# First attention of a two-layer kernel: the next batch's key pieces placed in odd steps only, two or three in a row

## The reference, cut to what matters

```
def _L0_xattn_ref(x, y, ...):                       # y = ctx, x = layernorm(x)
    y_dca, y_main = y[:, -16:, :], y[:, :-16, :]
    k_dca = _ln(...); v_dca = ...                   # from y_dca @ Wkv_dca
    q = _ln((x @ Wq + bq).reshape(b, s1, 16, 16), qn_w, qn_b)
    k = _ln(y_main @ Wk + bk per head, kn_w, kn_b); v = y_main @ Wv + bv
    ctx     = softmax(q k^T * 0.25) v               # 16 heads of 16
    ctx_dca = softmax(q k_dca^T * 0.25) v_dca
    return (ctx + ctx_dca) @ Wo + bo
```

## Time and profile before

| what | value |
|---|---|
| median of three runs | 1445.93 us |
| profiled execution, its own time | 1445.58 us |
| its span, first to last instruction | 1444.2 us |
| mean granted TensorE clock | 0.956 |
| PE busy | 1328.7 us (92%) |
| DVE busy | 1083.1 us (75%) |
| ACT busy | 894.2 us (62%) |
| POOL busy | 700.1 us (48%) |

### The profile page before, as it was taken

One profiled execution on the slowest core, in us unless ns is written; L12 is line 12 of the kernel. 1 busy time (PEld: TensorE's weight loads), 2 busy tenths in 40 slices (PEclk: granted clock), 3 DMA queues, 4 the chain that ended last, 5 costly groups with the idle time before them and its releaser, 6 DMA issues.

```text
span 1444.2 us, 25271 instructions
## 1 busy us (share of the span) xinstructions
PE 1328.7 (92%) x8652; PEld 646.2 (45%) x8652; DVE 1083.1 (75%) x2323; ACT 894.2 (62%) x1575; POOL 700.1 (48%) x785
## 2 busy tenths in 40 slices
PE   5798998889889899789999999999999999999999
PEld 4343444344333344335454544445454545454445
DVE  6767788688797357767877776967778888888766
ACT  4746756657765756466666666656665556656554
POOL 4036243334140046157655557665577565556643
PEclk9788998999989999899999999999999999999999
DMA  4000400301250100001000000000010000000000
GB/s 179 1 1 5 84 8 14 57 2 20 52 206 1 60 1 7 23 24 30 1 1 1 23 2 24 6 1 24 1 30 30 1 30 1 30 1 1 1 2 30
DMA packets 20486, 36.68 MB, mean 25 GB/s; under 512 B 4898, under 2 KB 15238, under 8 KB 19334
## 3 DMA queue, kind: packets, MB, share of 16 engines
q1 hardware_dynamic: 20358, 35.07, 8.3%
HBM read 26.53 MB, written 1.15 MB: 19 GB/s over the span
## 4 chain that ended last, share of the span: by engine, by line
PE 48%; DVE 4%; issue 3%; ACT 2%; POOL 2%; DVEq 0%; POOLq 0%; ACTq 0%
PE BK L740 47%; DVE arena L1715 2%; POOL arena L2178 1%; ACT arena L2014 1%; PE BK L1391 1%; DVE arena L2367 0%; DVE arena L2373 0%; DVE BK L1740 0%; ACT arena L2026 0%; ACT L1034 0%; POOL arena L1117 0%; POOL arena L2169 0%; PE BK L1064 0%; ACT arena L2399 0%; POOL arena L1115 0%
## 5 line engine op out<-in xcount | busy, mean ns | idle before, releaser
L740 PE MATMUL BK<-arena 128*128 128x512 bf16 (+11 forms) x8322 | 1286.2, 359 | 72.4 <-DVE arena L1553 21.1
L740 PEld LDWEIGHTS BK<-arena 128*128 128x128 bf16 (+7 forms) x8322 | 612.1, 104 | 709.4 <-issue 206.8
L2178 POOL TENSOR_TENSOR arena<-arena 128x512 bf16<-128x512 f32 (+1 forms) x416 | 441.9, 1067 | 226.9 <-ACT arena L2014 175.3
L2014 ACT ACTIVATE arena<-BK,arena 128x512 f32<-128x512 f32 (+1 forms) x416 | 285.7, 687 | 186.8 <-PE BK L740 183.0
L1910 ACT ACTIVATE arena<-BK 128x512 f32<-128x512 f32 (+1 forms) x416 | 222.8, 601 | 108.4 <-PE BK L740 106.0
L1553 DVE TENSOR_REDUCE arena<-BK 128x1 f32<-128x512 f32 x384 | 240.7, 681 | 51.2 <-PE BK L740 50.6
L1740 DVE TENSOR_TENSOR BK<-BK,arena 128x512 f32<-128x512 f32 (+1 forms) x352 | 243.7, 692 | 16.1 <-ACT arena L2014 10.4
L1715 DVE CUSTOM_DVE_ANT_0 arena<-BK,arena 128x512 bf16<-128x512 f32 (+1 forms) x256 | 147.0, 574 | 102.4 <-PE BK L740 99.2
L2026 ACT ACTIVATE arena<-BK 128x512 bf16<-128x512 f32 (+1 forms) x256 | 129.5, 508 | 90.0 <-PE BK L740 88.8
L1766 DVE SCALAR_TENSOR_TENSOR arena<-BK,arena 128x256 f32<-128x256 f32 x128 | 55.8, 476 | 15.0 <-PE BK L740 15.0
L2077 POOL TENSOR_TENSOR arena<-arena 128x1024 f32<-128x1024 f32 (+2 forms) x15 | 23.3, 1551 | 89.1 <-DVE arena L1495 89.1
(11 more groups left out here) (188 smaller groups left out, 888.0 us busy)
## 6 DMA issues: line engine op xcount, KB each, us to landing
arena<-arena SPq DMA_DIRECT2D x144, 50.0 KB, 2.2
arena<-in_ctxT SPq DMA_DIRECT2D x8, 800.5 KB, 4.6
arena<-in_ctxk SPq DMA_DIRECT2D x4, 768.0 KB
arena<-in_wo SPq DMA_DIRECT2D x1, 2048.0 KB, 7.5
arena<-in_wqT SPq DMA_DIRECT2D x1, 2048.0 KB, 8.7
arena<-in_x SPq DMA_DIRECT2D x4, 256.0 KB, 9.9
arena<-in_rsel SPq DMA_DIRECT2D x1, 1024.0 KB, 9.6
arena<-in_rw1T SPq DMA_DIRECT2D x1, 1024.0 KB, 5.2
```

The lines of the kernel that those rows point to most:

```text
L740: return T.matmul(out_, lhsT, rhs, start=start, stop=stop, skip_group_check=True)
L2014: A.activation(P1[k][0:m, :], BK[i][0:m, :], ACT.Exp, scale=SCALE1, bias=mcb[0:m, b, kt:kt + 1]).then_inc(free[i], 1)
L2178: G.tensor_tensor(Pl[k][0:m, :], P1[k][0:m, :], Ph[k][0:m, :], ALU.subtract).then_inc(p_low, 1)
```

## The change

The pieces of `keyed` are given in odd steps only. A quota grows by 1.5 per step up to step 29 and by 1 afterwards; odd steps spend all of it. Steps 1 to 29 so take three pieces each instead of two, and the even ones none instead of one; from step 30, two and none instead of one and one. The number of pieces given by the end of each odd step is what it was.

```
+        quota = 0
         for s in range(-LEAD0, 16 * NKT + LAG0):
...
                 b = s // 52
-                for _ in range(1 + s % 2 if s < 30 else 1):
+                quota += 1.5 if s < 30 else 1
+                while quota >= 1 and s % 2 == 1:
+                    quota -= 1
                     next(keyed, None)
                 if b + 1 < B and s % 6 == 3:
                     next(valued[b + 1], None)
```

## The result

The changed kernel takes 1452.26 us (median of 20 runs, 1446.73 to 1454.68), the kernel before in the same session 1441.43 us (20 runs, 1436.9 to 1449.38). The ratio, which is taken from the means, is 1.0065, 95% interval 1.0053 to 1.0078: some 9.4 us slower, between 7.6 and 11.2 (the medians lie 10.8 us apart). The prediction was +0.7 us, no change. Executions of one and the same kernel lie several us apart, so a single profile shows where time goes, and only many runs show how much.

What follows compares the result with a forecast made beforehand. PE was taken as the bound (busy 92% of the span), with DVE full in some windows. -5.3 + 2.5 + 1.5 + 1.5 + 0.5 = +0.7 us gave 1446.6 us; range 1440.6 to 1452.8, the forecast's own 1443.5 to 1449.

Steps and rivals of the forecast that it cites:

- Rival (c): Slower: PE reaches group 7 no earlier, something else replacing the wait for rows; +6.0 us, 1451.9 us; chance 0.05.
- (b): Faster: seven banks let PE run over late ACT or DVE, losses cost 1 instead of 6.0 us; 1441.6 us; chance 0.26.
- credit for the clock behind it: Behind group 7's removed stall, 4.32 us at clock 0.50 would run at 1.00, saving 2.2 us.
- part 2: Batch 1, three key tiles in a row: PE's stalls at steps 24 and 30 grow, +2.5 us.
- part 4: Root steps behind `oD` delay the row maxima PE waits for: +1.5 us in batch 3, +0.5 in batch 2.
- part 3: Paired key tiles: step 80's slip counted at group 7; batch 3's SP chain shifts, group 11's wait grows, +1.5 us.
- part 1: Batch 2: six key DMAs go behind group 7's bounce, so PE's wait and half clock there vanish, -5.3 us.
- nothing else: Instructions unchanged in number and size; `kk`, `q`, `qr` move where PE is full; bank shifts cost nothing, +-1 us.
- Rival (a): Slower: longer stalls at steps 24, 30 and 109 bring half clock, 5 to 7 us, near 1452 us; chance 0.27.
- its own mark: Two of steps 24, 30 and 109 show clock 0.50 over some 4 us that were at 1.00 before.

Runs made afterwards that it cites:

- `nw 3 2` alone: Kernel before with only one root step, three DVE instructions, moved from ahead of `oD` to behind it (steps 108 and 109): 1444.36 us, ratio 1.002.
- kernels without SP's backlogs: Second-half key DMAs of batches 2 and 3 held behind group 7's and 11's bounces: on the kernel before 1431.51 us (0.9929), on the changed kernel 1445.6 us (1.0028).

## Why the prediction was right or wrong

**The number.** The measured 1452.26 us lies within the stated range, 1440.6 to 1452.8, and outside the forecast's own, 1443.5 to 1449. That the wide range holds it is luck: the range was built on 1445.93 us, and counted from the 1441.43 us of the 20 runs it would end near 1448. The forecast, no change, did not come true: the kernel is 9.4 us slower.

**What held.** Which stalls the change touches, and their lengths, came out point by point: SP's order with its 42 DMAs, the end of group 7's wait, and 2.71, 3.16, 2.48 and 3.86 us for the stalls that it said would grow. The 4.60 us for group 11's rows is the number that it gave, but kernels with the old order there have it too. Rival (c), a wait that stays at group 7, fell, and so did (b): no bank hid any of it.

**The step that failed: pricing a longer stall by its own length.** The sum gave the removed stall a credit for the clock behind it, 2.2 us, and gave the added ones no such charge. The kernels with one part each show the size of that:

| term | predicted | stall grew by | measured |
|---|---|---|---|
| part 2, batch 1's key tiles | +2.5 | 2.4 | 5.8 us (3.0 to 8.5) |
| part 4, batch 3's root steps (104 to 115) | +1.5 | 1.8 | 4.9 us (2.7 to 7.1) |
| of these, `nw 3 2` alone | +1.3 | 1.4 | 2.9 us (0.1 to 5.5) |
| part 3, batch 3's tiles | +1.5 | not shown | 3.5 us (1.2 to 5.8) |
| part 1, group 7 | -5.3 | -3.7 | -2.7 us (-5.0 to -0.4) |

Each loss is some two to three times what it was priced at, and the gain is half. In the first two rows the predicted value lies clearly outside the interval, in the last one just outside, and in the two between inside. The kernels without SP's backlogs say the same of the whole: 14.1 us, where parts 2 to 4 had been put at 6.0. The gain also overlaps with part 3's stall in step 80, as the prediction had it. The five parts that do not overlap (0.50, -0.05, -0.19, 0.34 and 0.24%) add up to 0.84%, the whole change is 0.65%; each is known to 0.2% at best, so this is no contradiction.

PE's busy and idle time over the same steps, with the same matmuls to within a few records, shows how a stall comes to cost more than its length. In steps 104 to 120 the changed kernel's trace is 5.7 us longer: 4.0 of it is PE's busy time (35.53 in place of 31.52 us), and 1.7 is idle time. With `nw 3 2` alone it is 1.4 busy and 2.0 idle, in steps 16 to 36 with the key tiles alone 1.7 and 3.6.

**How regular half clock is behind a wait.** The granted clock of all 14 traces, at the places where PE's wait differs between kernels (half clock that begins in the wait or within 3 us of its end):

| place | wait, us | half clock behind | shorter wait, us | half clock behind |
|---|---|---|---|---|
| step 30, last key copy | 3.16 to 3.17 | 6 of 6 traces | 1.81 to 1.82 | 0 of 8 |
| step 80, last key copy | 1.42 to 1.43 | 4 of 5 | 0.17 | 0 of 9 |
| group 7's rows | 3.54 to 4.53 | 6 of 6 | 0 to 0.82 | 0 of 8 |
| group 9's `mm` | 3.70 to 3.96 | 4 of 4 | 2.57 to 2.58; 0.44 to 0.74 | 3 of 8; 0 of 2 |
| group 11's rows | 3.68 to 6.27 | 11 of 11 | none | 0 of 3 |

So at these places a lengthened stall did bring half clock with it in all but one trace, and a shorter one seldom did. It lasts 3.4 to 10.2 us there. No one length of the wait divides the two: 1.43 us was enough in step 80, and 1.82 was not in step 30.

**A second, smaller miss is "nothing else".** Next to the stalls named, PE's wait in step 108 is 1.67 in place of 1.00 us, and it is 1.66 with steps 104 to 115 alone, so it comes of the change. The 1.71 us in step 116 for the next stage's norm (L1030) does not by itself: both kernels with batch 1's new order alone have it, with the old lists there, behind the half clock shown above.

**Rival (a) gave the time, 1452, and met its own mark.** It was to decide once two of three places showed half clock where it was full: the place behind step 30 and the one behind step 110 do; behind step 24 it was half before as well. Its mechanism is the one the table bears out, but its number is in part luck: its 5 to 7 us, counted from 1441.43, give 1446 to 1448. It had 0.27 where it deserved more, because one row was held against it: a single 1.82 us stall with 1.00 behind it. That row speaks for stalls of 1.82 us at that place, and not for 3.16.

**What stays open.** That half clock stands behind the longer stalls is shown. That it is the cause of the whole excess is not. Over the runs, the median of the mean clock is 0.958 for the changed kernel (20 runs) and 0.964 for the one before (79), and within either kernel an execution whose mean clock is lower by 0.01 is 5 to 6 us longer. By that line, an estimate, some 4 us of the difference go with the mean clock and some 6 are left at an equal one. (The two full profiles, 0.957 and 0.956, show no such difference, since the second is from an execution 4 us above its kernel's median.) And with extra matmuls in the waits the clock behind group 9 was full again while the time stayed. The Trainium skill (TensorE: Matmul & The Clock Gate, section "HAM oscillation — how this bites in real kernels") has work start cold behind each wait for a transfer. The rows agree behind the rows of groups 7 and 11, in all 17 waits of 3.5 us and more. The waits for ACT and DVE, with half clock behind 3.16 and 3.96 us, are not of that kind; nor was the 1.82 us wait of step 30, so that it did not disagree, as the prediction says it did. But 1.67 us was followed once by 0.68 and once by 1.00, the 36 matmuls took 5.48 us behind an unchanged 1.00, and 2.58 us was followed by half clock in three traces of eight. What sets these apart could not be read from the lists.

Steps 0 to 16 are a rival that no run settles. None of the five traces with the new order there has the 34.3 us that five of the nine with the old order have. If the new order makes that start rarer, it is a cost that is not a stall of its own; the runs put what batch 1's other steps cost at 1.4 us, within the noise.

## What to carry to other kernels

A stall added to an otherwise full PE cost about two to three times its length here (5.8 us for 2.4, 4.9 for 1.8); a removed one gave between 0.7 and 1.3 times its length (2.7 us for 3.7, 10.2 for 8.0). Give every lengthened stall the same clock charge that a removed one is credited with. Small pieces that share an engine with a critical reduction did better spread evenly: bunching them moved no work and lost 0.65%. And look for a small, urgent transfer that stands behind a long row of bulk ones on the same queue (48 DMAs, 33 us): issuing it behind half of them, in two places, gave 0.7%, more than all else tried.

## What the hardware showed that was not expected

Tiny DVE operations can take as long as a large one of POOL. The kernel before, one DVE line twice, beside POOL's row of five operations (7.74 us, some 1.5 us each), and PE's wait for DVE:

```profile
214.90 7.74 POOL L2092 TENSOR_TENSOR arena<-arena 128x512 f32<-128x512 f32 x5 [14.04 <-DVE arena L992]
...
215.94 1.93 DVE L987 TENSOR_TENSOR arena<-arena 128x2 f32<-128x2 f32 x1
...
222.30 6.74 PE L740 MATMUL BK<-arena 64*128 64x512 bf16 x42 [4.27 <-DVE arena L1553]
...
222.76 0.14 DVE L987 TENSOR_TENSOR arena<-arena 128x2 f32<-128x2 f32 x1
```

The same 128x2 operation takes 1.93 us beside POOL and 0.14 us without. The changed kernel has the same at this place (1.93 us at 220.00), so it is no part of the difference. This agrees with the Trainium skill (SBUF — State Buffer, section "Who interferes with whom"), where a DVE instruction with two SBUF inputs contends with a GpSimd instruction that reads SBUF, its second input coming through a read port that the two share. Three such operations in a row, 5.6 us, stand ahead of the maxima for which PE waits 4.27 us, one of its longest waits here, and moving them was not tried.
